# A macaron transformer block on one core: the attention's bound as the exponential's bias, and the first head begun earlier

## The reference, cut to what matters

```python
x = x + 0.5 * ffn(layernorm(x))          # rows quantised to FP6 in blocks of 32, times a quantised weight
x = x + attn(layernorm(x))
x = x + 0.5 * ffn(layernorm(x))
# attn, 16 heads of 8 features:
scores = Q @ K.T / sqrt(8) + 0.3 * log(sigmoid(val[head]) + 1e-6)   # the mask is the same for all batches
out = softmax(scores) @ V @ Wo + bo
```

## Time and profile before

| | us |
|---|---|
| Median of 3 runs | 846.21 (844.81 to 848.28) |
| Profiled execution, time | 850.78 |
| Its span in the trace | 848.9 |
| PE, ACT, DVE, POOL busy | 736.3, 648.6, 540.4, 193.2 |
| First and last exponential of the attention begin | 124.7, 808.6 |

### The profile page before, as it was taken

One profiled execution on the slowest core, in us unless ns is written; L12 is line 12 of the kernel. 1 busy time (PEld: TensorE's weight loads), 2 busy tenths in 40 slices (PEclk: granted clock), 3 DMA queues, 4 the chain that ended last, 5 costly groups with the idle time before them and its releaser, 6 DMA issues.

```text
span 848.9 us, 12809 instructions
## 1 busy us (share of the span) xinstructions
PE 736.3 (87%) x4337; PEld 259.6 (31%) x4337; DVE 540.4 (64%) x1382; ACT 648.6 (76%) x773; POOL 193.2 (23%) x163
## 2 busy tenths in 40 slices
PE   0565738898999999989899999999999999999996
PEld 0143311322233323332323234223331232331175
DVE  8977877556989737997676446675342346532245
ACT  1568597787888887877788888888888888888841
POOL 0405672003443212263022021342030002000010
PEclk9986957999999999999999999999999999999998
DMA  5539558996767675765956746687758555556301
GB/s 148 113 123 350 204 148 317 326 243 200 222 206 231 205 202 176 189 207 120 272 159 206 227 126 208 194 227 228 204 193 226 188 166 172 176 175 208 96 1 55
DMA packets 56076, 162.10 MB, mean 191 GB/s; under 512 B 14130, under 2 KB 24506, under 8 KB 45586
## 3 DMA queue, kind: packets, MB, share of 16 engines
q1 hardware_dynamic: 51780, 154.37, 59.6%
q0 software_dynamic: 1776, 5.93, 2.1%
q10 hardware_dynamic: 2446, 0.89, 0.5%
HBM read 117.86 MB, written 43.29 MB: 190 GB/s over the span
## 4 chain that ended last, share of the span: by engine, by line
PE 48%; DVE 17%; ACT 15%; issue 9%; DMA 6%; SPq 3%; POOL 1%; DVEq 0%; ACTq 0%; POOLq 0%
PE S_PS L1756 18%; PE O_PS L1774 17%; ACT BIG L819 12%; DVE S_PS L1282 6%; DMA BIG<-shift_rows 6%; PE F_PS L1655 3%; SPq L430 2%; SPq L433 1%; PE R_PS L1784 1%; PE P_PS L1692 1%; DVE ST L1007 1%; PE F_PS L1645 1%; PE P_PS L1696 1%; ACT BIG L877 1%; PE P_PS L1645 1%
## 5 line engine op out<-in xcount | busy, mean ns | idle before, releaser
L819 ACT ACTIVATE BIG<-S_PS 128x1024 f32<-128x1024 f32 x512 | 505.2, 1023 | 116.8 <-PE S_PS L1756 113.7
L1756 PE MATMUL S_PS<-BIG 98*128 98x512 bf16 x1024 | 307.3, 390 | 43.0 <-DVE S_PS L1282 14.1
L1774 PE MATMUL O_PS<-BIG,VXP 128*18 128x512 f32 (+2 forms) x2048 | 271.7, 604 | 0.0
L1282 DVE COPY S_PS<-BIG 128x512 f32<-128x512 f32 x256 | 159.8, 687 | 175.6 <-ACT BIG L819 173.4
L1756 PEld LDWEIGHTS S_PS<-BIG 98*128 98x128 bf16 x1024 | 79.1, 98 | 299.8 <-ACT BIG L819 138.6
L645 POOL TENSOR_TENSOR XDT<-PART 128x512 bf16<-128x512 f32 x24 | 29.0, 1206 | 315.1 <-ACT PART L782 315.1
L1774 PEld LDWEIGHTS O_PS<-BIG,VXP 128*18 128x18 f32 (+2 forms) x2048 | 34.3, 95 | 101.5 <-issue 94.2
L620 POOL TENSOR_TENSOR X<-X,BFH 128x512 f32<-128x512 f32 x16 | 24.1, 1525 | 146.2 <-ACT BIG L853 113.1
L870 ACT ACTIVATE BIG<-S_PS,TEMP 128x1024 f32<-128x1024 f32 x32 | 34.3, 1111 | 20.7 <-PE S_PS L1947 20.4
L661 POOL TENSOR_TENSOR PART<-PART 128x512 bf16<-128x512 f32 x28 | 37.1, 1325 | 29.9 <-DVE PART L1190 29.9
L620 POOL TENSOR_TENSOR BIG<-BIG,BFH 128x512 f32<-128x512 f32 x16 | 20.9, 1332 | 98.5 <-DVE BIG L1107 84.4
(11 more groups left out here) (212 smaller groups left out, 758.6 us busy)
## 6 DMA issues: line engine op xcount, KB each, us to landing
BIG<-ln_masks SPq DMA_DIRECT2D x62, 1024.0 KB, 6.8
ln_masks<-BIG SPq DMA_DIRECT2D x16, 1024.0 KB, 6.2
BIG<-q_parts SPq DMA_DIRECT2D x63, 192.0 KB
BIG<-k_parts SPq DMA_DIRECT2D x63, 144.0 KB
BIG<-q_parts SPq DMA_DIRECT2D x63, 128.0 KB
q_parts<-PART SPq DMA_DIRECT2D x9, 768.0 KB, 3.8
k_parts<-PART SPq DMA_DIRECT2D x18, 384.0 KB, 4.5
BIG<-k_parts SPq DMA_DIRECT2D x63, 96.0 KB
```

The source lines that it names most:

```text
L819: act.activation(E[:, m % 2, j, 2 * pair:2 * pair + 2, :], S_PS[:, pair, :, :], ACT.Exp, scale=LOG_WEIGHT)\
L1282: ve.tensor_copy(S_PS[:, pair, i, :], LNM[:, slot, 2 * pair + i, :]).then_inc(s["seeded"], 1)
L1756: mm = pe.matmul(S_PS[:, pair, i, :], KT[0:ALL_ROWS, slot, K_COL[j], 128 * kb:128 * kb + 128], QT[0:ALL_ROWS, slot, j, :], start=False, st ...
L1774: mm = pe.matmul(O_PS[32 * j:32 * j + ahead + HD + 1, :], VXP[:, slot_of(n), at - ahead:at + HD + 1], E[:, m % 2, j, kb, :], start=kb == 0 ...
```

## The change

Four parts. First, the bound becomes one number for each batch and head: the largest norm of q times the largest norm of k. HSEL is widened so that two products put both sums of squares into one 32-row tile; DVE takes the maxima (TOP), ACT their logarithms, DVE spreads them on a matrix DIAG of 32x16 that adds the two logarithms of a head, PE multiplies by ones, ACT takes the exponential of half of it, and DVE makes of it the column SHIFT. ACT then adds that column in the exponential, as its bias. The two extra rows of the stack, their stores and their loads go. Second, the first head's stack is loaded by SP in two pieces, the one for batches 0 and 1 before masks 9 and 10 are stored, the other behind them, and POOL loads nothing. Third, the logarithms of masks 13, 14 and 15 are taken at the beginning of heads 1, 2 and 3. Fourth, the flag is worked out at the beginning of the tail, SP tests it once, before it waits for the last stores; in the last quantisation ACT takes its Ln and Exp one centring earlier, and one bias addition of POOL waits. Some ticks move by up to three.

```diff
-LIFT, MAX_BOUND = 200.0, 200.0
+LIFT, MAX_BOUND, MARGIN = 200.0, 200.0, 1.02
...
+LN_IN_HEADS = {1: 13, 2: 14, 3: 15}
+
...
+CHAINS = ((43, 58, 75, 91), (3, 27, 51, 83), (3, 27, 51, 91), ())
+CLOSE = dict(norm_ve=-2, turn_pe=3, xnt_act=3, q_pe=4, q_act=4, hi_q_ve=6, mid_q_ve=11, k_pe=9, k_act=9, hi_k_ve=10,
+             mid_k_ve=17, norms_pe=15, top_ve=17, top_act=19, diag_ve=19, v_pe=13, v_ve=14, bound_pe=21, bound_act=21,
+             row_ve=23)
+APART = dict(norm_ve=-2, turn_pe=0, xnt_act=0, q_pe=4, q_act=6, hi_q_ve=6, mid_q_ve=9, k_pe=12, k_act=13, hi_k_ve=17,
+             mid_k_ve=18, norms_pe=17, top_ve=18, top_act=19, diag_ve=21, v_pe=21, v_ve=22, bound_pe=23, bound_act=24,
+             row_ve=26)
 SECOND = (CLOSE, APART, APART, {})
 LAST = ({},
         dict(turn_pe=(10, 17, 25, 31), at_act=(10, 18, 26, 34), out_pe=(12, 20, 28, 36), add_ve=(13, 21, 29, 37),
```

```diff
+        def load_first_stack(engine, more):
+            if more:
+                parts_stored(engine, 0)
+            else:
+                for e in range(2):
+                    engine.wait_ge(s[f"first_out_q{e}"], 16)
+                    engine.wait_ge(s[f"first_out_k{e}"], 16 * len(K_COLS_OF[e]))
+            name, kc, qc = ("first_more", slice(1, K_COLS), slice(2, QB)) if more else ("first_stack", slice(0, 1), slice(0, 2))
+            head = slice(HD * head_of(0), HD * head_of(0) + HD)
...
+                rows = slice(PART_ROWS * a, PART_ROWS * b)
...
-
-
+            lnm_stored(sp, 1)
+            lnm_stored(sp, 2)
+            sp.wait_ge(s["zeros_out"], 16 * 2)
+            load_first_stack(sp, False)
+
+            store_mask(9)
+            store_mask(10)
+            load_first_stack(sp, True)
             load_stack(sp, 1)
-            store_mask(9)
-            load_shift(sp, 1)
-            for h in range(10, 13):
-                store_mask(h)
+            store_mask(11)
...
                 store(NQ - 1, j)
-            sp.wait_ge(s["out_sent"], 16 * B)
+
             sp.wait_ge(s["flag_ready"], 2)
...
+            def top_ln(n, j, size=1):
+                c = calls_of_bounds(n, j)
+                act.wait_ge(s["top"], 2 * (n * QB + j + size))
+                act.wait_ge(s["top_diag"], c)
+                act.activation(TOP[:, j:j + size], TOP[:, j:j + size], ACT.Ln).then_inc(s["top_ln"], 1)
+
+            def bound_exp(n, j, size=1):
...
+                act.wait_ge(s["bound_row"], 3 * c)
+                act.activation(SHIFT[:, n % 2, j:j + size, :].rearrange("p j h -> p (j h)"), R_PS[:, 0:NH * size], ACT.Exp, scale=0.5)\
+                   .then_inc(s["bound_exp"], 1)
 
...
                 if pair == 0 and m == 1:
                     lnm_stored(act, 9 + j)
+
                 if k == 0 and m == 0:
-
-                    parts_stored(act, 0)
+                    act.wait_ge(s["first_out_q1"], 16 * QB // 2)
+                if k == 2 and m == 0:
+                    act.wait_ge(s["first_out_k1"], 16 * sum(len(c) for c in K_COLS_OF[1::2]))
                 if j == 0 and m >= 2:
                     act.wait_ge(s["pv_done"], T * (m - 2) + 2 * pair + 2)
-                act.activation(E[:, m % 2, j, 2 * pair:2 * pair + 2, :], S_PS[:, pair, :, :], ACT.Exp, scale=LOG_WEIGHT)\
+                act.activation(E[:, m % 2, j, 2 * pair:2 * pair + 2, :], S_PS[:, pair, :, :], ACT.Exp, scale=LOG_WEIGHT,
+                               bias=SHIFT[:, n % 2, j, head_of(m):head_of(m) + 1] if is_short(n) else 0.0)\
                    .then_inc(s["e_ready"], 1)
 
```

```diff
+                    if k == 0 and m in LN_IN_HEADS:
+                        ln_mask(LN_IN_HEADS[m])
                     exp_step(m, k)
...
                 if i == BOUNDS_AT:
-                    first_bound_exp()
+                    top_ln(0, 0, QB)
+                if i == BOUNDS_AT + 1:
+                    bound_exp(0, 0, QB)
             for q in range(NQ):
...
-            for j in range(QB):
+            for j in range(QB - 1):
                 last_centre(j)
             lnexp(NQ - 1, 2, 0)
...
+            def top(n, j):
                 g = n * QB + j
-                ve.wait_ge(s["norms_k"], g + 1)
-                c = Count(ve, "k_top", 2 * g)
-                c(ve.tensor_reduce(KTOP[:, :], (O_PS if n == 0 else R_PS)[0:NH, :], AX.X, ALU.max))
-                c(ve.tensor_scalar(KDIAG[:, :], IDENT[0:NH, 0:NH], KTOP[:, 0:1], None, ALU.mult))
-
...
+            def top_diag(n, j, size=1):
+                c = n * QB + j - QB + 1 if past(n) else 0
+                ve.wait_ge(s["pairs_made"], 3)
+                ve.wait_ge(s["top_ln"], c + 1)
+                ve.wait_ge(s["bound_psum"], c)
+                TT(DIAG[:, j:j + size, :], PAIRS[:, None, :].to_broadcast((2 * NH, size, NH)),
+                   TOP[:, j:j + size, None].to_broadcast((2 * NH, size, NH)), ALU.mult).then_inc(s["top_diag"], 1)
+
+            def bound_row(n, j, size=1):
+                b = n * QB + j - QB + 1 if past(n) else 0
+                ve.wait_ge(s["bound_exp"], b + 1)
                 c = Count(ve, "bound_row", 3 * b)
-                c(ve.tensor_scalar(BROW[:, :, :], BOUND[:, :, :], -1.0, LIFT, ALU.mult, ALU.add), wait=False)
-                c(ve.tensor_reduce(BMAX[:, 1:2], BOUND[:, :, :], AX.XY, ALU.max))
-                c(TT(BMAX[:, 0:1], BMAX[:, 0:1], BMAX[:, 1:2], ALU.max))
```

```diff
-                pe.matmul((O_PS if n == 0 else R_PS)[0:NH, :], HSEL[:, :], SQR[:, 1, :], start=True, stop=True)\
-                  .then_inc(s["norms_k"], 1)
-
-
...
+            def bound_product(n, j, normed, size=1):
+                c = n * QB + j - QB + 1 if past(n) else 0
+                pe.wait_ge(s["top_diag"], c + 1)
+                pe.wait_ge(s["bound_exp"], c)
                 if past(normed):
...
                 j, pair, slot = k // 2, k % 2, m % 2
                 if k == 0:
-                    pe.wait_ge(s[stack_name(m)], K_LOADS * (m // 2 + m % 2) if m else FIRST_LOADS)
-                    pe.wait_ge(s["ones_set"], 1)
-                    if m == 0:
-                        pe.wait_ge(s["first_shift"], 16 * T)
+                    pe.wait_ge(s[stack_name(m)], K_LOADS * (m // 2 + m % 2) if m else K_LOADS)
+                if m == 0 and k == 4:
```

More of the change, by code:

```diff
@@ L603, in _ @@
                 sp.wait_ge(s["rows_zeroed"], 16 * 3)
-            general_path(sp, general)
-            sp.wait_ge(s["flag_ready"], 2)
-            with sp.If(sp.value_load(FLAG[0:1, 0:1], min_val=0, max_val=1) > 0):
+                for n in range(NQ, 2 * NQ):
+                    general(n)
                 sp.wait_ge(s["out_sent"], 16 * 2 * B)
+            sp.wait_ge(s["out_sent"], 16 * B)
         @block.gpsimd
@@ L1253, in first_bounds_rows @@
[L1253 to L1270 removed]
+                ve.wait_ge(s["norms"], g + 1)
@@ L1737, in turn_first_bounds @@
[L1737 to L1741 removed]
+                pe.matmul(R_PS[:, 0:NH * size], ONES[:, :], DIAG[:, j:j + size, :].rearrange("p j h -> p (j h)"),
+                          start=True, stop=True).then_inc(s["bound_psum"], 1)
```

329 lines of the change are left out of this document (116 added, 213 removed).

## The result

The change made the kernel slower, by less than one per cent: 853.57 us (median of 13 runs, 848.48 to 862.93) against 848.28 (13 runs of the kernel before on the same chips). The ratio is 1.0068, with a 95% interval of 1.0037 to 1.0099. I had forecast 838 and given slower a chance of 0.16; the time lies outside my range of 827 to 850. The profiled execution took 854.11 us, with a span of 851.2.

What follows compares the result with a forecast made beforehand. It took the heads as a ping-pong of PE's products and ACT's exponentials, neither full, with DMA limiting 125 to 205. Terms -9.3 + 2 + 3 - 5 - 2 - 6 - 3.1 + 12 = -8.4 gave 838 us, range 827 to 850.

Steps and rivals of the forecast that it cites:

- Start of the attention, -9.3: Ahead of the first exponential: three logarithms (5.7 us), shorter bound work (0.7) and PE's KDIAG waits (2.9) save 9.3 us.
- lies beside a logarithm of 1.9 us: In the bound's chain at the start: DVE's spread, product and three small instructions run beside a 1.9 us logarithm.
- Second half of the stack, +2: In head 0: the first stack's second half lands at 120.3 but PE wants it at 118.5; +2 us, bounds 0 and +6.
- logarithms +3: Beginning of heads 1 to 3: each moved logarithm costs 1 us after ACT's idle time, +3 us in all.
- early loads -5: Heads between 124 and 205: masks 9 and 10 stored earlier and no seventh issue cut PE's load waits by 5 us.
- the start gives back what it won: Rival: the earlier attention meets DMA engines at 0.90 and waits as before; 843.2 us, no change; chance 0.18.
- Later shift loads, -2: Three later heads that waited for loads: only the seventh issue, 0.64 us and its gap, goes; -2 us, bounds 0 and -4.9.
- Chains, -6: Twelve background chains: lighter ACT and DVE work and no KDIAG wait save 0.5 us each, -6 us, bounds 0 and -12.
- Tail, -3.1: End of the program: flag instructions off the end 0.5 us, one flag test 2 us, earlier quantisation scales 0.6; together -3.1 us.
- Bias, +12: Attention's 512 exponentials: the bias column adds 0.09 us each, three of eight on a clean head's path; +12 us overall.
- ACT becomes the bound: Rival: in the step loop, longer exponentials make PE wait at every step, 0.5 us a head, 32 us; 857.7 us; chance 0.14.
- the free bias: Rival: the exponentials' bias column costs nothing or ACT's idle time takes it up; 826 us as a median; chance 0.15.

Runs made afterwards that it cites:

- the additions moved: Changed kernel with POOL's four additions of the bias to x at the start waiting until the bound is worked out: 859.51 us, ratio 1.0103.
- the form without bias and with masks held back: Changed kernel without the exponentials' bias, mask loads of heads 24, 27, 40, 43 waiting for scores two heads earlier: 838.66 us, ratio 0.9900.
- the kernel before with the late store: Kernel before, third quarter's bound stores of batches 1 and 2 one head later, behind the loads of masks 40 and 43: 853.50 us, ratio 1.0079.
- the one with the mask stores: Changed kernel, POOL's additions waiting for the bound and masks 9 and 10 stored behind the first stack's second half: 862.93 us, ratio 1.0191.

## Why the prediction was wrong, step by step

- **Start of the attention, -9.3: wrong.** It was -2.6. Two steps failed. Behind the first of the last eight logarithms I had forecast 6.4 us (5.7 for the three logarithms, 0.7 for the bound). It was 2.4, and 6.2 with the additions moved (from 16.4 to 10.1). The step that failed there is that DVE's part of the chain "lies beside a logarithm of 1.9 us". The other 2.9, for PE's waits for KDIAG ahead of these logarithms, were not there either: the first of them starts at 108.09 in place of 108.30. I had priced DVE's instructions by their own length, and not asked what POOL does at that time once its loads have gone. Its additions moved 6 us forward and held DIAG for 4 us. The Trainium skill says it ("SBUF — State Buffer", section "SBUF: two separate sides"): VectorE and GpSimd share one pair of ports as an exclusive lock, for which a VectorE instruction with two SBUF inputs must wait until a GpSimd instruction that reads SBUF has ended. The rows agree, 4.06 us beside the additions and 0.20 without, and go further: the product was held not for one instruction but through the rest of four.
- **Second half of the stack, +2, logarithms +3, early loads -5: wrong as a sum of separate terms.** These are one limit, the loads and stores that have to pass between 110 and 205. What is won at one wait appears at the next: the first exponential was moved from 10.1 to 19.7, and head 8 came between 103.2 and 105.2 all the same (108.7 in one run), but at 100.0 with half of the masks' bytes, one trace. The rival "the start gives back what it won" had this mechanism, with a chance of 0.18, and I sized it too small; besides, halfway between -8.4 and +5.9 is -1.3, not the -3 that I used for it.
- **Later shift loads, -2: wrong, +4.6 in heads 38 to 41.** I counted the seventh issue of 0.64 us and forgot what the removed store did by standing in the queue: it held back a transfer of 1 MB that competes with the stack. The experiments show it in both directions, 3.9 and 3.5 us in heads 38 to 41; the other 0.7 of the 4.6 are not explained.
- **Chains, -6: too large; 2.5 are shown.** In heads 8 to 63 the form without bias and with masks held back gains 6.2 us on the kernel before. But 2.5 of them are in the 43 heads that repeat, and 4.6 in heads 22 to 30, less 0.8 lost in heads 38 to 41. In heads 22 to 30 the kernel before with the late store, the same program there, took 99.5 in place of 103.7, so that gain is in the waits for stacks and not shown to be the chains'.
- **Tail, -3.1: about right, -2.6.** From the last exponential to the end it is 37.7 us against 40.3. From the last exponential to the last residual it is 33.1 in both, so the earlier logarithm of the quantisation brought nothing, and all of it is at the end: 4.6 us behind the last residual against 7.2.
- **Bias, +12: right.** 1.11 us, 9.95 us for a clean head, and 12 us for the whole by two pairs (12.3 and 12.4 by the medians, 11.5 and 11.9 by the ratios). In part that is luck: I had scaled by 192 waits of PE for the exponential, and the changed kernel has 263. The bound's rival (ACT becomes the bound, 32 us) was wrong; the free bias was wrong too.

Put together from the traces of the two kernels: -4.9 at head 8, -2.2 in heads 22 to 30, -2.5 for the chains and -2.6 for the tail are 12.2 us of gain, where I had forecast 20.4. Against them stand 4.6 for heads 38 to 41 and the bias, 9.8 in the 43 heads that repeat. That is +2.2, and the span shows +2.3; the first two gains are no larger than what such heads differ between traces of one program. So the bias was priced right, and the change lost because two fifths of the gains weren't there and a cost was that I had not seen.

What stays open: heads 0 to 7 differ by up to 5.5 us between traces of programs that are the same there, and heads 22 to 30 by up to 4 us in the kernel before. The early masks of heads 24 and 27 are one part of it in the changed kernel; what decides the rest, I didn't find. Of the single edits to the start (POOL's additions, the mask stores, the logarithms) the medians are 4 to 9 us above the changed kernel's, though by head 8 they were at most 2 us behind. Only the one with the mask stores is slower beyond its interval, and its cause wasn't tried; in the other two traces the longer time lies in heads 22 to 37.

## What to carry to other kernels

A removed instruction does two things besides its own time: what stands behind it in its queue comes earlier, and what it was waiting for no longer holds them back. List both for every queue that the change touches, ask which engine or transfer they now run beside, and above all where 1 MB transfers stand behind a small one. Where a stretch shows DMA engines at 0.9, treat it as one limit of bytes, and don't add up the waits in it one by one. An operand that costs 0.09 us in the instruction with the largest share is not hidden by idle time on average; count how many of them stand in the chain of a clean period. Here three of eight in each of 64 heads would be 17 us, and 12 were measured.

## What the runs showed of the hardware

- A DVE product of two SBUF operands, 32x64, took 4.06 us while POOL made additions on 128x512 back to back, and 0.20 us without them. It was held through the rest of four POOL instructions, not of one.
- The bias column costs 91 to 92 ns on each exponential of 128x1024 from PSUM (1023 to 1114 and 1115), whether the column is a constant or worked out.
- A store of 384 KB let its waiter go 6.8 us after its issue with two stores of 1 MB issued 1.5 us ahead of it in another queue, and 3.0 us after without them.
